# Recurrent message passes of a graph network: the reset-gated term is added on TensorE by an identity matmul, and the first message pass is reordered

## The reference, cut to what matters

```
out = h = relu(n_feat @ lin0_w.T + lin0_b)
w_e = (relu(e_feat @ en1_w.T + en1_b) @ en2_w.T + en2_b).reshape(-1, 32, 32)   # one 32x32 matrix per edge
for _ in range(6):
    msg = einsum('ei,eio->eo', out[src], w_e)
    m = relu(segment_sum(msg, dst) + conv_bias)
    r = sigmoid(W_ir m + W_hr h + b)
    z = sigmoid(W_iz m + W_hz h + b)
    n = tanh(W_in m + b_in + r * (W_hn h + b_hn))
    h = out = (1 - z) * n + z * h
```

## Time and profile before

| | before |
|---|---|
| median of 3 runs | 7569.24 us |
| lowest, highest | 7554.29, 7577.0 us |
| the profiled execution: its time | 7563.81 us |
| its span in the trace | 7561.7 us |
| P5 in the trace | from 2605 to 3075 us |
| P6 to P10 in the trace | from 3088 to 5065 us |
| an interval between two scans of full blocks, P5 | 34.2 to 35.7 us |
| the same, P6 to P10 | mostly 27.3 to 27.5 us, now and then 26.5 us |

### The profile page before, as it was taken

One profiled execution on the slowest core, in us unless ns is written; L12 is line 12 of the kernel. 1 busy time (PEld: TensorE's weight loads), 2 busy tenths in 40 slices (PEclk: granted clock), 3 DMA queues, 4 the chain that ended last, 5 costly groups with the idle time before them and its releaser, 6 DMA issues.

```text
span 7561.7 us, 70665 instructions
## 1 busy us (share of the span) xinstructions
PE 5467.3 (72%) x20759; PEld 2497.0 (33%) x20765; DVE 4597.3 (61%) x6813; ACT 2487.6 (33%) x4074; POOL 3548.0 (47%) x3814
## 2 busy tenths in 40 slices
PE   1896888444568755686767676866675796999998
PEld 1443444223233322222222222223354542434343
DVE  5465333123446577697979797883475644666666
ACT  1564333111223311111111121213321254666665
POOL 3677773667655453453535363636206566600000
PEclk9997888665558777798989898987797898999999
DMA  5001555232457588686868687871101001000000
GB/s 167 12 10 46 199 204 205 74 87 79 117 134 175 143 280 296 216 315 227 317 231 314 223 321 245 300 257 42 42 1 28 18 16 27 27 19 25 20 20 20
DMA packets 572067, 1039.67 MB, mean 137 GB/s; under 512 B 112303, under 2 KB 306500, under 8 KB 570789
## 3 DMA queue, kind: packets, MB, share of 16 engines
q1 hardware_dynamic: 458724, 976.22, 37.6%
q0 software_dynamic: 112960, 58.94, 4.6%
HBM read 828.11 MB, written 222.61 MB: 139 GB/s over the span
## 4 chain that ended last, share of the span: by engine, by line
PE 40%; DVE 19%; issue 15%; POOL 13%; DMA 7%; ACT 5%; SPq 1%; DVEq 0%; POOLq 0%; ACTq 0%
POOL gathered L887 10%; DVE ring L2198 5%; PE ps L1407 5%; PE ps L1039 5%; PE ps L1101 5%; PE ps L1189 3%; PE ps L1190 2%; DMA ring<-net 2%; DVE blocks L2198 2%; PE ps L1194 2%; POOL edge_rows L1021 2%; PE ps L1162 2%; DVE w L2245 1%; DVE ring L2240 1%; PE ps L1530 1%
## 5 line engine op out<-in xcount | busy, mean ns | idle before, releaser
L887 POOL DMA_INDIRECT gathered<-table,idx_slot x2156 | 2099.7, 974 | 1090.5 <-issue 548.7
L2198 DVE TENSOR_TENSOR ring<-ring,ps 128x1024 f32<-128x1024 f32 (+2 forms) x1008 | 1058.3, 1081 | 245.1 <-DMA ring<-net 198.2
L1101 PE MATMUL ps<-ring,mats 128*32 128x512 f32 (+2 forms) x4032 | 677.2, 630 | 409.7 <-DVE ring L2198 327.1
L1039 PE MATMUL ps<-mats,gathered 128*128 128x128 f32 x1029 | 204.6, 338 | 594.5 <-DMA gathered<-table,idx_slot 551.3
L879 POOL COPY idx_slot<-idx_row 128x16 int32<-128x16 int32 (+2 forms) x154 | 32.1, 209 | 1118.9 <-SPq L592 1080.8
L1101 PEld LDWEIGHTS ps<-ring,mats 128*32 128x32 f32 x4032 | 155.4, 122 | 896.2 <-issue 565.9
L2265 DVE SCALAR_TENSOR_TENSOR x_block<-ps,bias,blocks 128x512 f32<-128x512 f32 x300 | 224.6, 749 | 366.0 <-PE ps L1194 365.7
L1194 PE MATMUL ps<-ring,wts 128*128 128x512 f32 x600 | 344.4, 657 | 124.8 <-ACT blocks L1771 124.6
L1407 PE MATMUL ps<-w,en 128*128 128x512 f32 (+2 forms) x896 | 381.0, 585 | 0.0
L1039 PEld LDWEIGHTS ps<-mats,gathered 128*128 128x128 f32 x1029 | 136.1, 168 | 741.2 <-DMA gathered<-table,idx_slot 588.9
L1189 PE MATMUL ps<-ring,wts 128*128 128x512 f32 x600 | 334.9, 641 | 40.1 <-ACT ring L1785 31.4
(11 more groups left out here) (310 smaller groups left out, 11886.9 us busy)
## 6 DMA issues: line engine op xcount, KB each, us to landing
ring<-net SPq DMA_DIRECT2D x792, 512.0 KB, 3.9
blocks<-net SPq DMA_DIRECT2D x264, 512.0 KB
net<-ring SPq DMA_DIRECT2D x176, 512.0 KB, 2.9
gathered<-table,idx_slot POOLq DMA_INDIRECT x2352, 3.5
ring<-net SPq DMA_DIRECT2D x144, 256.0 KB, 2.9
table<-w SPq DMA_DIRECT2D x143, 256.0 KB, 2.7
ring<-d_sp SPq DMA_DIRECT2D x100, 256.0 KB, 4.3
x_sp<-x_block SPq DMA_DIRECT2D x79, 256.0 KB
```

The source lines that it names most:

```text
L887: pool.indirect_dma_start(dests(k), None, rows, bass.IndirectOffsetOnAxis(ap=dst[:, k:k + 1], axis=0)).then_inc(done, 16)
L1039: last = nc.tensor.transpose(dst[:, k * P:k * P + P], src[:, k * P:k * P + P], mat["ident"])
L1101: last = mm(message[t * D:t * D + D, 0:wd(i)], adders[2 * m + c], ring[slot][:, c * wd(i):(c + 1) * wd(i)], start=(m == 0 and c == 0), sto ...
L2198: v.tensor_tensor(pair, pair, state, ALU.mult).then_inc(sig["pr"][S_], 1)
```

## The change

Three things. In P6 to P10 the addition of `sum_new` is taken from DVE. PE leaves the accumulation of W_in m open (`stop=False`) and adds r times hidden by a matmul of tile w3 with the identity (`gru_sum`), and ACT's tanh reads the bank. The bank `pA[S_]` is then free only when tanh has read it, so that the signal waited for is `n` and no longer `npre`. In the same passes `gru_hidden` of space D moves ahead of the sums m = 2, and DVE's gate of space D moves from k = 15 to k = 13. In P5 the steps between the products move: the sum and the scale from k = 0 and 1 to k = 3, the residual from 2 to 4, the norm's steps from 8, 9, 10, 13 to 7, 8, 9, 11; on PE the variances move ahead of the sums m = 1, and the norm's spread ahead of the sums m = 2.

```diff
@@ PE, P5
                 edge_sums4(q, i, 0)
                 if more:
                     conv_norm(q, i + 1, centre)
+                    conv_norm(q, i + 1, variances)
                 edge_sums4(q, i, 1)
                 if more:
-                    conv_norm(q, i + 1, variances)
+                    conv_norm(q, i + 1, scales)
                 edge_sums4(q, i, 2)
                 if more:
-                    conv_norm(q, i + 1, scales)
                     conv_lin(q, i + 1)
                     copies4(q, i + 1)
                 edge_sums4(q, i, 3)
@@ PE, P6 to P10
             def gru_head(q, i):
...
-                bank_read(q, "npre", S_, i)
+                bank_read(q, "n", S_, i)
...
                 if u == D_:
-                    bank_read(q, "npre", D_, i)
-                mm(fit(pA[S_], i), wt["in"], fit(w[0][u], i), start=True, stop=True).then_inc(sig["gin"][u], 1)
+                    bank_read(q, "n", D_, i)
+                mm(fit(pA[S_], i), wt["in"], fit(w[0][u], i), start=True, stop=False)
...
+            def gru_sum(q, u, i):
+                pe.wait_ge(sig["rh"][u], q.n("rh", u, i) + 1 + CREDIT)
+                mm(fit(pA[S_], i), mat["ident"], fit(w[3][u], i), start=False, stop=True).then_inc(sig["npre"][u], 1)
...
                         gru_hidden(q, S_, i + 1)
                     edge_sums4(q, i, 1)
                     if more:
+                        gru_sum(q, S_, i + 1)
                         gru_reset(q, D_, i + 1)
                         gru_update(q, D_, i + 1)
+                        gru_hidden(q, D_, i + 1)
                     edge_sums4(q, i, 2)
                     if more:
-                        gru_hidden(q, D_, i + 1)
+                        gru_sum(q, D_, i + 1)
                         copies4(q, i + 1)
                     edge_sums4(q, i, 3)
@@ ACT, P6 to P10
-                gru_new(q, u, i)
+                act.wait_ge(sig["npre"][u], q.n("npre", u, i) + 1 + CREDIT)
+                f(fit(w[1][u], i), fit(pA[S_], i), ACT.Tanh, bias=one_col("in")).then_inc(sig["n"][u], 1)
@@ DVE, P5
-                return {0: lambda: conv_sum(q, i), 1: lambda: conv_scale(q, i), 2: lambda: conv_add(q, i),
-                        8: lambda: norm_variance(q, conv_space, i), 9: lambda: norm_root(q, conv_space, i),
-                        10: lambda: norm_refine(q, conv_space, i), 13: lambda: norm_apply(q, conv_space, i, [fit(x, i) for x in conv_out])}
+                return {3: lambda: (conv_sum(q, i), conv_scale(q, i)), 4: lambda: conv_add(q, i),
+                        7: lambda: norm_variance(q, conv_space, i), 8: lambda: norm_root(q, conv_space, i),
+                        9: lambda: norm_refine(q, conv_space, i), 11: lambda: norm_apply(q, conv_space, i, [fit(x, i) for x in conv_out])}
@@ DVE, P6 to P10
-                    return {8: lambda: (gate(q, S_, i, one_bank[0]), sum_new(q, S_, i, one_bank[1])),
+                    return {8: lambda: gate(q, S_, i, one_bank),
                             10: lambda: (blend_a(q, S_, i, blk(h[S_], i)), blend_b(q, S_, i)),
                             11: lambda: blend_c(q, S_, i, blk(h[S_], i), "hs"),
-                            15: lambda: (gate(q, D_, i, one_bank[0]), sum_new(q, D_, i, one_bank[1]))}
+                            13: lambda: gate(q, D_, i, one_bank)}
```

More of the change, by code:

```diff
@@ L228, in plan @@
     for k in range(6, 5 + STEPS):
-        add(f"P{k}", "hs m gin npre" + GRU, s="head" + MSG, times=K16, alternate="ld_gs")
+        add(f"P{k}", "hs m npre" + GRU, s="head" + MSG, times=K16, alternate="ld_gs")
         add_tab(f"T{k}")
@@ L1639, in _ @@
                     gru_hidden(q, u, 0)
+                    gru_sum(q, u, 0)
                 copies4(q, 0)
@@ L2656, in _ @@
                 q = p_[name]
-                one_bank = (pB[S_], pB[S_]), (pA[S_], pA[S_])
+                one_bank = pB[S_], pB[S_]
                 def gru_step(q, i):
-                    return {8: lambda: (gate(q, S_, i, one_bank[0]), sum_new(q, S_, i, one_bank[1])),
+                    return {8: lambda: gate(q, S_, i, one_bank),
                             10: lambda: (blend_a(q, S_, i, blk(h[S_], i)), blend_b(q, S_, i)),
                             11: lambda: blend_c(q, S_, i, blk(h[S_], i), "hs"),
-                            15: lambda: (gate(q, D_, i, one_bank[0]), sum_new(q, D_, i, one_bank[1]))}
+                            13: lambda: gate(q, D_, i, one_bank)}
                 def own_step(q, i):
@@ L2668, in _ @@
                 steps = gru_step(q, 0)
-                for run in (steps[15], own_step(q, 0)[3], steps[8], steps[10], steps[11]):
+                for run in (steps[13], own_step(q, 0)[3], steps[8], steps[10], steps[11]):
                     run()
```

## The result

The changed kernel takes 7541.07 us (median of 20 runs, 7522.27 to 7553.79) against 7561.99 us (20 runs, 7547.33 to 7581.31) of the kernel before, run beside it: ratio 0.997, 95% interval 0.9961 to 0.9979. That is 21 us less, where 95 us less was forecast: the sign was right, the size less than a quarter of it, and the time lies 1 us above the range.

What follows compares the result with a forecast made beforehand. DVE was taken to bound P6 to P10, and no unit to be full in P5. Gains of 48 us (P6 to P10) and 47 (P5) from 7563.8 gave 7469, or 7474 against the runs' median; range 7430 to 7540.

Steps and rivals of the forecast that it cites:

- P6 to P10, what is removed: In P6 to P10, leaving out space S's addition takes 0.72 us per block off DVE's path.
- The addition of space D: In P6 to P10, removing it brings nothing if copies stay slow: -0.72 us, but D's gate costs +0.67 uncovered.
- The copies and the clock: In P6 to P10, PE idles 1.3 us before the copies, not 2.24, so they run at full clock: -1.22 us per block.
- Rival 1: The half clock stays at the copies, so P6 to P10 give about 0: 7522 us, chance 0.14.
- step (3): In P6 to P10, later sums m = 2 delay the load for the next k = 0: +0.3 us per block, bounds 0 and 0.9.
- The waits at k = 8 and for the transposes: In P5, DVE's waits of 3.38 us for the load of k = 8 and 1.20 for the transposes both go.
- The wait for the variances: In P5, a new DVE wait at k = 7 until D's variances are there: 1.6 to 1.9 us a block.
- the DMA term: In P5, 0.9 us a block added to DVE's 29.35 for the DMA engines and held-back loads, making 30.2.
- SP's holding back: In P5, SP holds the next block's ring loads until the residual's store lands and four x and d loads are issued.
- Rival 2: P5 is held by the DMA engines or the chain centre to sums m = 1 at 32.2 us: 7496 us, chance 0.15.
- rival 3: In P6 to P10, sums m = 2 come late on PE, 2.6 us at half clock, +1.6 a block: 7603 us, chance 0.06.
- both together: Half clock stays at the copies and P5 is held at 32.2 us a block: 7544 us, chance 0.05.

Runs made afterwards that it cites:

- half_after: The changed kernel with each ring load cut to half its bytes (256 KB), the second half left unloaded: 7396.12 us, ratio 0.9777 to the kernel before.
- mixed: hidden_late with space D's addition back on DVE at k = 15, the identity sum kept for S alone: 7497.23 us, ratio 0.9928 to the kernel before.
- hidden_late: The changed kernel with gru_hidden of D back behind the sums m = 2 and D's gate at k = 14: 7497.25 us, ratio 0.9925.
- sp_order: hidden_late with P5's loads of x and d issued after the next block's ring loads k = 0 to 3: 8205.21 us, ratio 0.9933 to the kernel before.
- half_before: The kernel before with each ring load cut to half its bytes (256 KB), the second half left unloaded: 7511.56 us, ratio 0.9943.
- late_again: hidden_late unchanged, run again later as the base for others on one chip: 8343.35 us, ratio 0.9946 to the kernel before at 8397.93.

## Why the prediction was right or wrong

**P6 to P10, what is removed: right.** `half_after` has the block at 26.0 us where the terms without the load (-0.72, +0.67, -1.22) gave 26.1. The addition of S is gone from DVE's path. Between the two kernels with half the bytes it is 27.34 less 26.01: 1.33 us a block, forecast 1.27 without loads.

**The addition of space D: right.** By itself it brings nothing; `mixed` takes the time of `hidden_late`.

**The copies and the clock: right in the block, in another way than I put it.** The gap of 1.22 to 1.23 us (forecast 1.3) and the full clock came in 49 of 55 blocks. Rival 1, the half clock at the copies, fell. The clock was lost again elsewhere: 13 sums at half clock, after gaps of 2.0 to 3.9 us, where PE waits for products that wait for loads (`hidden_late` has 5 such sums). I had followed the clock at one place of the block and not at the others. The Trainium skill (TensorE: Matmul & The Clock Gate, Part 1) calls the moment at which the clock rises after a kernel's start run-variable, from one run of a kernel to the next. The rows show the like within one execution: after one and the same gap of 2.24 us the copies before the change took 1.14 us, 2.09, or a time between.

**"What the waits behind it cost", step (3): this step failed.** The mechanism was named, and rightly placed (in the good block above the sums m = 2 end at 10.04 us behind k = 7, predicted 10.1; k = 0 starts at 14.05, predicted 14.05). The size was not. I took +0.3 us a block for the waits for loads, with 0.9 as the upper end; what the runs show is the mean block of 27.35 us less the 26.01 of `half_after`, +1.3. The prediction said that the waits at k = 0 and k = 8 don't add up within one block. They do in part: in 22 of 50 full blocks both a load before k = 0 and that of k = 0 are waited for (0.5 us on average ahead of a k = 0 that waits, 1.2 us ahead of one that doesn't). By the sums of DVE's idle time, changed kernel against `half_after`, k = 0 has 0.45 us a block more (81.0 us in 45 intervals for 60.6, loads and copies together), which is near the 0.3. The loads of k = 8 to 10 have another 0.35 and those of other steps 0.19, where the sum had nothing. The rest is in DVE's busy time, 24.76 us a block for 24.56, and in smaller waits.

I also reckoned with the median landing of 3.9 us as if each load had it. In P7 (3600 to 3800 us) the median went from 3.8 to 4.2, and the longest was 5.9 before and 6.1 after: late loads had been there before, and had had slack. A late load delays a product and thereby the sums, some of these once more by the half clock, and thereby the next four loads. How the loss divides among lateness, spread and half clock wasn't separated. Taking `gru_hidden` out from ahead of the sums m = 2 gives back 23 us by the times and 33 by the profiles; with the gate's move it is 39, of the 48 forecast.

**P5: right in what goes, short by one term.** The waits at k = 8 and for the transposes are gone. The wait for the variances is 0.7 us a block, mostly one of 0.4, not 1.6 to 1.9. Without half of the transfers a block is 29.0 us, against 29.35 by my sum without DMA. With them it is 32.2: the DMA term is 2.8 to 3.2 us and not 0.9, and this is the second term that was mis-sized. SP's holding back is a cause of it, as I wrote: it makes the wait of 3.4 us at k = 0, and 2.2 us of that stay even with half of the bytes. Taking it away (`sp_order`) shortens P5 by 1 to 6 us in all, so that it isn't the bound. I had also taken the landing of 3.9 us from P7; in P5 (2700 to 3000 us) the median was 4.9 before the change and 4.3 after. My lower end of the gain (32.2 us, the share of P7) was the right value. Sizes: P5 -31.5 us timed, forecast -47. That the transfers come in bursts, with a hole while the sums m = 0 run at half clock, is in the rows; that this, and not the share as such, sets the 32.2 us wasn't tested.

**The rivals.** Rival 2 (P5 held at 32.2) came true as to P5. P6 to P10 ended at about 0, as in rival 1, but by a milder form of rival 3: the sums m = 2 late on PE, by `gru_hidden`'s 0.86 us at full clock and not by 2.6. Its sign, over 1 us of waiting for the ring at k = 0, is there in 34 of 50 full blocks. The case "both together", 7544 at a chance of 0.05, has the number, by luck, and not the mechanism. What its chance lacked is that both halves hang on the same thing, a load stream with little slack left, so that they can fail together. In the sum I let the DMA engines reach a share of 0.94 in P5 (28.3 of 30.2) and 0.92 in P6 to P10 (0.88 of 27.49 in 26.4); the five blocks of P5 reached 0.88, the stretch below 0.88, and the better kernel 0.90.

The same stretch, 3500 to 3800 us, by window, in the changed kernel and in `hidden_late`:

```profile
3500.00:3800.00 300.00, 245.91 (x1142) 81.80 (x1140) 267.37 (x275) 58.75 (x88) 156.25 (x169) 0.98 0.88 312
```

```profile
3500.00:3800.00 300.00, 249.52 (x1189) 83.77 (x1188) 274.51 (x284) 60.21 (x91) 157.68 (x170) 0.99 0.90 321
```

## What to carry to other kernels

When an engine that bounds a loop gets faster, first look at what feeds it: with the DMA engines at a share of 0.88 and the ring's slots freed by another engine, the next bound was less than 1 us away, and the waits for several loads of a block add up. A load's landing should be taken with its spread, not with its median. Whatever frees a buffer (here the sums on PE) should stand ahead of all that can wait, since 0.9 us of unrelated work ahead of it cost 0.6 us in each block. Rivals that hang on the same resource are one rival, with the chance of one.

## What the runs showed of the hardware

A load that moves half as much does not land in half the time: 2.7 us in the median for 256 KB (`half_before`), 3.8 to 4.2 for 512 KB (before and after), in P7.

The clock's dependence on the gap is a matter of frequency. In the full blocks of P6 to P10 gaps before the copies of 1.2 us were followed by the half clock (copies of about 2.0 us or more) in 5 of 47 cases in the changed kernel, gaps of 2.2 to 2.3 us in 21 of 47 in the kernel before and in 38 of 50 in `half_before`, with some in between. With the gap of 1.2 us and half of the bytes (`half_after`) it was none of 50.

The same kernel takes 7557 to 7562 us in the first sets of runs and 8270 or 8398 in the later ones, and 7557 and 8270 were measured on a chip of the same number. One kernel was traced in both: `hidden_late` with a span of 7493 us and `late_again` with 8339. Of the 846 us 450 come before P5 and 207 after P10, 20 in P5 and 169 in P6 to P10. There 24 us are added between the last scan of a pass and the first of the next (74 us in place of 50), where tables are stored and gathered again, and the full blocks are 27.7 us long in place of 26.7. So the part in which the change works differs as well. What causes it stays open.
